# Moving the dt chain of a state-space scan four to six units ahead in the engines' orders, and adding the skip term on VectorE instead of TensorE

## The reference, cut to what matters

```
dt = softplus(dt_in @ dt_proj_w.T + dt_proj_b)        # 2048 time steps, 1024 channels
dA = exp(dt[..., None] * A)                           # 16 states of each channel
dBx = (dt * x_full) * B                               # the drive of each state
h = dA * h + dBx                                      # scan over time, 16 states a channel
y = sum over the 16 states of C * h  +  D_skip * x_full
y = y * silu(z);  out = y @ out_proj_w.T
```

## Time and profile before

| | us |
|---|---|
| median of 3 runs | 2795.44 |
| lowest and highest | 2795.18, 2797.02 |
| the profiled execution, own time | 2799.06 |
| its span | 2797.3 |
| mean granted clock of TensorE | 0.96 of full |
| first scan to the first scan of group 31 | 54.8 to 1000.4 |

### The profile page before, as it was taken

The page is one execution under the profiler, slowest core; times in us unless marked ns, Lnnn a source line. Parts: engine busy times, 40 slices in busy tenths (PEclk is TensorE's granted clock), DMA queues, the critical chain, the costliest instruction groups (busy, mean ns, idle before and its releaser), DMA issues.

```text
span 2797.3 us, 32656 instructions
## 1 busy us (share of the span) xinstructions
PE 2618.7 (94%) x11152; PEld 1877.7 (67%) x11160; DVE 2082.0 (74%) x2656; ACT 1191.1 (43%) x1786; POOL 1285.8 (46%) x868
## 2 busy tenths in 40 slices
PE   7888888898889879999999999999999999999999
PEld 4443444454345337888888778788878788888887
DVE  5999899999999976543376677777877865555553
ACT  5655555555555635422254543343333422222221
POOL 4899899899999961210001023123222422222220
PEclk9999899899899879999999999999999999999999
DMA  7754655555465437121111112112111121111111
GB/s 248 220 165 129 180 150 139 166 158 148 125 182 160 132 113 266 54 76 53 62 51 61 40 44 69 46 46 68 46 39 46 45 53 46 51 48 50 49 46 68
DMA packets 152311, 275.37 MB, mean 98 GB/s; under 512 B 27344, under 2 KB 27856, under 8 KB 151632
## 3 DMA queue, kind: packets, MB, share of 16 engines
q1 hardware_dynamic: 152144, 273.27, 32.7%
HBM read 178.01 MB, written 61.34 MB: 86 GB/s over the span
## 4 chain that ended last, share of the span: by engine, by line
PE 66%; DVE 9%; issue 8%; POOL 8%; ACT 4%; DMA 3%; SPq 1%; POOLq 0%; DVEq 0%; ACTq 0%
PE ps L1757 19%; PE ps L1759 19%; PE ps L1758 19%; DVE state L1401 4%; POOL read L1233 4%; PE ps L1806 3%; PE ps L1822 3%; ACT ps L896 1%; DMA vpack<-vl 1%; DMA b_d<-ev 1%; PE ps L1966 1%; POOL dt_t L1197 1%; POOL sp_rest L1182 1%; PE ps L1940 1%; DMA uraw<-y_d 1%
## 5 line engine op out<-in xcount | busy, mean ns | idle before, releaser
L1233 POOL TENSOR_TENSOR read<-state,c_t 128x512 f32<-128x512 f32 x512 | 662.9, 1316 | 74.4 <-DVE state L1401 35.8
L1401 DVE TENSOR_TENSOR_SCAN state<-ps,drive 128x512 f32<-128x512 f32 x512 | 622.5, 1216 | 4.2 <-ACT ps L896 1.7
L1295 POOL TENSOR_TENSOR wdeq<-packed,scales 128x1024 f32<-128x1024 f16 x96 | 256.2, 2668 | 800.7 <-DVE packed L1530 800.7
L1757 PE MATMUL ps<-xh,ghi 128*128 128x512 f32 x1536 | 607.3, 395 | 0.0
L1759 PE MATMUL ps<-xh,glo 128*128 128x512 f32 x1536 | 598.0, 389 | 0.0
L1758 PE MATMUL ps<-xl,ghi 128*128 128x512 f32 x1536 | 597.8, 389 | 0.0
L896 ACT ACTIVATE ps<-ps,a_exp 128x512 f32<-128x512 f32 x512 | 337.2, 661 | 385.4 <-PE ps L1806 383.9
L1392 DVE TENSOR_TENSOR drive<-ps,b_t 128x512 f32<-128x512 f32 x512 | 344.2, 672 | 53.6 <-PE ps L1806 49.5
L1697 DVE TENSOR_TENSOR act_o<-act_o,ps 128x512 f32<-128x512 f32 x192 | 131.8, 686 | 284.6 <-PE ps L1759 283.2
L1153 ACT ACTIVATE ahi<-act_o 128x512 fp32r<-128x512 f32 x192 | 121.6, 633 | 520.6 <-DVE act_o L1697 520.6
L1757 PEld LDWEIGHTS ps<-xh,ghi 128*128 128x128 f32 x1536 | 288.4, 188 | 62.6 <-issue 3.1
(11 more groups left out here) (197 smaller groups left out, 3842.0 us busy)
## 6 DMA issues: line engine op xcount, KB each, us to landing
whi<-w_d SPq DMA_DIRECT2D x63, 256.0 KB, 4.9
wlo<-w_d SPq DMA_DIRECT2D x63, 256.0 KB, 5.5
b_d<-ev SPq DMA_DIRECT2D x32, 256.0 KB
dpack<-dh SPq DMA_DIRECT2D x64, 128.0 KB, 4.4
dpack<-dl SPq DMA_DIRECT2D x64, 128.0 KB, 2.3
b_t<-b_d SPq DMA_DIRECT2D x32, 256.0 KB, 5.4
vpack<-vh SPq DMA_DIRECT2D x64, 128.0 KB, 2.3
vpack<-vl SPq DMA_DIRECT2D x64, 128.0 KB, 2.4
```

What stands on the lines that cost most here:

```text
L1233: pool.tensor_tensor(read[:, n % RRING, :], state[:, n % SRING, :], c_t[:, g % 2, :], ALU.mult).then_inc(read_ready, 1)
L1295: pool.tensor_tensor(wdeq[:, :].rearrange("p (h n) -> p h n", h=2), codes, scale, ALU.mult).then_inc(deq, 1)
L1401: dve.tensor_tensor_scan(state[:, n % SRING, :], ps[:, decay_bank(n), :], drive[:, n % DRING, :], 0.0, ALU.mult, ALU.add)\
L1757: pe.matmul(out_, w_h, x_h, start=(start and k == 0), stop=False)
```

## The change

Three things move in the orders, and one is computed elsewhere.

- ACT: `dt_high(g + 1)` from c = 6 to c = 2, `v_high` from 8 to 4; `soft_abs` from 12 to 11, `soft_pos` from 13 to 12, `soft_exp` from 14 to 12, `soft_one` from 15 to 13, `soft_log` from 15 to 14.
- POOL: `soft_rest` from c = 0 of the group to c = 14 of the group before, `soft_sum` from 1 to 15 of the group before; `soft_dt` from 2 to 0, `dt_x` from 3 to 1, `dt_low` from 7 to 3, `v_low` from 9 to 5.
- SP: the loads of the packs now stand ahead of `weights_after(first + 1)`.
- The skip term: ACT's `skip_weights` and `take_y` and PE's matmul with `skip_w` are gone. DVE's `skip_y` computes D_skip * x + bank into `y_t` at c = 6 of the next group. The gather of m = 0 opens the bank.

```diff
@@ sync
-                if jobs:
-                    weights_after(first + 1)
                 if 0 <= g + 1 < STEPS:
                     load_pack_dt(g + 1)
                     load_pack_v(g + 1)
+                if jobs:
+                    weights_after(first + 1)
@@ scalar
                     decay(g, c)
-                    if c == 1:
-                        skip_weights(g)
-                    if g and c == 6:
-                        take_y(g - 1)
...
-                        if c == 6:
+                        if c == 2:
                             dt_high(g + 1)
-                        if c == 8:
+                        if c == 4:
                             v_high(g + 1)
                     if nb < B:
+                        if c == 11:
+                            soft_abs(g + 2)
                         if c == 12:
-                            soft_abs(g + 2)
+                            soft_pos(g + 2)
+                            soft_exp(g + 2)
                         if c == 13:
-                            soft_pos(g + 2)
+                            soft_one(g + 2)
                         if c == 14:
-                            soft_exp(g + 2)
-                        if c == 15:
-                            soft_one(g + 2)
                             soft_log(g + 2)
...
-            u_high(0)
-            take_y(STEPS - 1)
-            u_high(1)
+            for m in range(2):
+                u_high(m)
@@ gpsimd
+                    if g == 0 and c == 0:
+                        soft_rest(1)
+                        soft_sum(1)
                     if g + 1 < STEPS:
                         if c == 0:
-                            soft_rest(g + 1)
+                            soft_dt(g + 1)
                         if c == 1:
-                            soft_sum(g + 1)
-                        if c == 2:
-                            soft_dt(g + 1)
+                            dt_x(g + 1)
                         if c == 3:
-                            dt_x(g + 1)
-                        if c == 7:
                             dt_low(g + 1)
-                        if c == 9:
+                        if c == 5:
                             v_low(g + 1)
+                    if g + 2 < STEPS:
+                        if c == 14:
+                            soft_rest(g + 2)
+                        if c == 15:
+                            soft_sum(g + 2)
@@ vector
+            def skip_y(q):
+                i = q % CT
+                dve.wait_ge(gathered, 4 * (q + 1))
+                dve.wait_ge(x_t_loaded[q % 3], x_loads(q))
+                if q >= 2:
+                    dve.wait_ge(y_stored[q % 2], 16 * (q // 2))
+                dve.scalar_tensor_tensor(out=y_t[:, q % 2, :], in0=x_t[:, q % 3, :],
+                                         scalar=d_skip[:, i:i + 1], in1=ps[:, 4, :],
+                                         op0=ALU.mult, op1=ALU.add).then_inc(y_ready, 1)
...
+                    if g >= 1 and c == 6:
+                        skip_y(g - 1)
...
             u_low(0)
+            skip_y(STEPS - 1)
             u_low(1)
@@ tensor
-                if m == 0:
-                    pe.wait_ge(skip_ready, g + 1)
-                    pe.wait_ge(x_t_loaded[g % 3], x_loads(g))
-                    pe.matmul(ps[:, 4, :], skip_w[:, :], x_t[:, g % 3, :], start=True, stop=False)
                 for j in range(4):
                     last = pe.matmul(ps[32 * j:32 * j + 32, 4, :], gather[:, m, :],
-                                     read[:, (n + j) % RRING, :], start=False, stop=(m == 3))
+                                     read[:, (n + j) % RRING, :], start=(m == 0), stop=(m == 3))
```

More of the change, by code:

```diff
@@ L90, in build @@
     a_log = place("a_log", [P, P], F32, after())
-    skip_w = place("skip_w", [P, P], F32, offset_of["end"] - 4 * P)
     a_exp = place("a_exp", [P, P], F32, after())
@@ L282, in build @@
         gathered = sem("gathered")
-        skip_ready = sem("skip_ready")
         y_ready = sem("y_ready")
@@ L876, in v_high @@
                 act.activation(vh[:, :], v_t[:, :], ACT.Copy).then_inc(vh_ready, 1)
-            def skip_weights(q):
-                if q:
-                    act.wait_ge(gathered, 4 * q - 3)
-                i = q % CT
-                act.activation(skip_w[:, :], ident[:, :], ACT.Identity,
-                               scale=d_skip[:, i:i + 1]).then_inc(skip_ready, 1)
-            def take_y(q):
-                act.wait_ge(gathered, 4 * (q + 1))
-                if q >= 2:
-                    act.wait_ge(y_stored[q % 2], 16 * (q // 2))
-                act.activation(y_t[:, q % 2, :], ps[:, 4, :], ACT.Copy).then_inc(y_ready, 1)
             def decay(g, c):
```

## The result

The changed kernel takes 2821.0 us in the median (2819.0 to 2823.0 in 4 runs), the kernel before 2796.2 beside it: a ratio of 1.0087, with a 95% interval of 1.0070 to 1.0105. It is slower, by 24.8 us. The prediction said 2823.2, in a range of 2788 to 2842. The profiled execution took 2822.9 us; its span is 2821.1, against 2797.3.

A forecast was written before the change was run, and what follows sets the result against it. It took DVE to bound the scan stage, POOL close behind. Terms: +18.6 skip term, +29.2 net gap at scan 3, -20.7 gaps removed, +0.7 final copy: +27.8 us on 2795.44, so 2823.2, range 2788 to 2842.

The forecast's parts named there:

- skip term on DVE: One more DVE instruction in each of 31 groups of the scan stage, 0.60 us each: +18.6, upper bound 32.6.
- gap at scan 3: DVE's scan of unit 3 waits for `dh`, held by POOL's late `dt_t`: 1.55 us in plain groups, 52.3 in all.
- the gaps that stood there: Old DVE gaps taken in: 19.5 us at first units, 3.6 at group 5's drive 0 and two scans; 23.1 subtracted.
- drive of unit 10: DVE's gaps at this drive vanish, as the skip matmul goes and packs come earlier: -20.7 us with two crumbs.
- The rule that the two count as the larger: DVE's gaps at scan 3 and at the first units, counted from scan 14, add up to the larger one.
- the sign that I named for it: DVE's scan of unit 3 shows a gap of about 1.5 us in nearly every group, 4 to 6 in groups 5 and 30.
- The six gaps at the lower clock: Unit 10's drive in groups 5, 13, 21, 29, 30, 31: 8.0 us goes once PE has no skip matmul.
- The three long ones: Unit 10's drive in groups 7, 15 and 23, waiting for weights: 12.5 us goes with earlier packs and a slower stage.
- The wait for `dt_t`: ACT's wait for this POOL result grows from 10.2 us in 7 waits to some 110 to 130 in 30.
- Rival 1: No gap at scan 3, old gaps at first units and unit 10 go: -24.5 us, 2771; chance 0.12.
- rival 2: No gap at scan 3, but the clock's gaps at the first units stay: -1.4 us, 2794; chance 0.12.
- Rival 3: Scan 3's gap comes and idle PE falls to the lower clock, making unit 10's drive late: +20, 2843; chance 0.12.

The follow-up runs named there:

- e1: The kernel before with ACT's, POOL's and SP's new orders, the skip term left on PE and ACT: 2816.6 us, ratio 1.0068.
- e3: The changed kernel with `dt_high` at unit 4 instead of 2 and `v_high` at unit 6 instead of 4: 2797.0 us, ratio 0.9997.
- e12: The changed kernel with PE's gather of four reads one unit earlier (units 3, 7, 11, 15): 2831.4 us, ratio 1.0118.
- e6: The kernel before with the dt chain moved ahead on ACT and POOL, SP's old order and the skip term on PE kept: 2816.4 us, ratio 1.0075.
- e9: The kernel before with SP's order alone changed, the packs ahead of the stage's weights: 2819.9 us, ratio 1.0088.
- e7: The kernel before with ACT's, POOL's and SP's new orders, but `dt_high` at unit 4, `v_high` at 6, and PE's gather one unit earlier: 2773.7 us, ratio 0.9925.

## Why the prediction was right

Forecast and runs go by the stage, in us; what was late before at the places of the gap was 25.8 by the starts (27.5 at drive 2, less 5.8 in groups 0 and 2, plus the 4.1 at drive 0 and scan 7 in groups 5 and 30).

| step of the prediction | said | measured |
|---|---|---|
| skip term on DVE | +18.6 | +19.5 (30 x 0.65) |
| gap at scan 3, with what it takes in at drive 2 | 52.3 | 49.4, 4.4 of it in group 0 |
| less the gaps that stood there | -23.1 | -25.8 |
| drive of unit 10 | -20.7 | -22.8 |
| DVE's other rows and gaps | 0 | +0.7 |
| sum in the stage | +27.1 | +21.0 |

The stage holds 30 additions, not the 31 that the prediction put into it: that of group 31 lies behind its end. So does the gap of group 31 at unit 10 (1.76), which the 20.7 include. Of DVE's other rows the `wlo` took 2.6 more from start to start and those of `scale_x` and `split_lo` 1.3 less; nothing of this was forecast, and no run was made for it.

1. **The gap at scan 3.** Right in cause and size: 2.58 us from `dt_t` to the scan, and a plain group late by about 1.5 at drive 2 and scan 3 together. Its place was half right. I had "a gap of about 1.5 in nearly every group" at scan 3; of the 22 plain groups three have it there (13, 21 and 29, 1.3), twelve have 0.35 to 0.84 behind a late drive 2 (or, in group 1, alone), and in seven drive 2 alone is late, by 1.4. The rule that the two count as the larger gave the right sum, but the sign that I named for it was overdrawn. `e1` shows that the order alone makes it, `e3` that two units undo it, `e12` that it and the one at drive 2 count as the larger of the two. Group by group I erred both ways. Group 0 was 4.4, not 1.3: POOL's first read waits 12.45 us there for the load of C, and `dt_t` stands behind it in the new order, which I didn't follow into the stage's start. Groups 3, 5 and 30 were 1.2, 2.8 and 5.2, not 2.5, 4.5 and 5.9.

2. **The gaps that stood before.** I took the new gap by starts and the old ones by the idle column, which is short of them by some 0.08 each and shows nothing of the smallest; that made the forecast's stage too slow by 2.7 and, at unit 10, by 2.1. With the 2.9 by which the new gaps came out smaller, and 1.6 the other way in the first and last rows of terms, this is the 6 us by which the stage came out under its forecast. Outside the stage 2.8 us were added where I had 0.7, and the medians grew by 1.0 more than the spans of the profiled executions; that brought the total within 2.2 us of the number. The mechanism held, but this closeness is luck, not insight.

3. **Unit 10.** The six gaps at the lower clock go with the skip matmul: `e1` and `e6`, which keep it, have 1.74 to 1.76 there in groups 21 and 29. The three long ones go as foretold, but by only one of the two moves that I named. I said "with the packs out some 6 us earlier SP stores x as soon as ACT has it" and counted SP's order as part of it. `e6` shows that the move of the chain, with its earlier `dl` and `vl`, does it without SP's, and `e9` that SP's order alone costs 23.5 us. The size of the term was right, and its cause half wrong.

4. **The wait for `dt_t`.** 76.7 us instead of 110 to 130, in 31 waits. The decay of unit 2 comes late itself where drive 2 does (in group 9 it waited 3.24 for PE's spread), and what it is late by is taken off the wait; in `e12`, where drive 2 isn't late, the wait is 130.1.

5. **The rivals.** Rival 1 (no gap) and rival 2 (no gap, but the clock's at drive 2 stays) are what `e3` is: 2797.0, where rival 2 said 2794. They needed `dh` two units later. Rival 3, the lower clock more often: the stretch of 200 to 300 us has 0.81 in the changed kernel and the mean of 60 to 960 is 0.89 against 0.91, but the drive of unit 10 was late nowhere; and `e3`, without the gap, has 0.89 too, so the gap is not what lowers it. The sentence of the Trainium skill (TensorE: Matmul & The Clock Gate, What's actually happening) that activity releases the throttle points the same way as that small fall; it decided nothing here.

For the addition, the page Vector Engine (DVE) Microarchitecture Reference (the Trainium skill, Measured stream behaviour on trn2) has 1.0417 ns a column and about 75 ns for each instruction, an estimate of 0.61 us for 512 columns. The trace has 0.64 to 0.65.

## What to carry to other kernels

- To move a producer ahead, count the row of the engine that feeds it, instruction by instruction, from the last event that the order can't change. It says where the move stops paying; here `dh` two units later gave all 24 us back, and the groups with odd work pay first.
- An instruction on the engine that bounds a stage costs its time less the gaps it removes or fills. Remove other gaps first and the same edit costs more (by the runs 3 us on the kernel before and 12 on `e7`), so a price measured on one kernel doesn't carry to the next.
- Two gaps behind the same anchor, an event that neither edit moves, count as the larger. Removing one alone shows nothing, or lets the other grow; find what stands ahead of the waited-for instruction in its engine's row, and move that.

## What the runs showed of the hardware

- A row's idle number starts at the end of the row before, and rows of DVE overlap: 1.21 us long, 1.13 from start to start. At unit 10 of the kernel before 22 drives were late, by up to 4.6, and the column shows 10 of them; the other 12 were late by some 0.2 each and show nothing. The Trainium skill (Perfetto Trace Analysis, DVE / Act Engine Instruction) puts the reported end at the acknowledged write, behind the point from which the next one may fetch; the rows agree.
- The granted clock sat at its lower level (1.2 GHz, 0.50 in 566 to 570 us of the changed kernel as in 554 to 558 before) at the start of groups, and a gather took 1.94 us there; in `e3` the gather of unit 4 of the same group took 1.06, at the higher level. Of the orders tried none was without such stretches.
- That SP's order by itself would cost as much as the whole change was the largest surprise. The issuing queue, waiting for a late piece, held back all that stood behind it: in group 15 PE's wait for weights grew from 2.13 us to 3.02, and DVE's drive waited 6.07 instead of 4.17.
